# Two attention layers with routed experts on one core: VectorE subtracts the rotary products from batch 3 on

## The reference

```python
q = (x @ Wq + bq).reshape(Bx, Tx, NH, HD)      # 16 heads of 8
k = (x @ Wk + bk).reshape(Bx, Tx, NKV, HD)     # 4 heads of 8
x1, x2 = x[..., ::2], x[..., 1::2]             # rotary, for q and k
rot = concatenate([x1 * cos - x2 * sin, x1 * sin - x2 * cos], axis=-1)
scores = q @ k^T / sqrt(8), causal; softmax; @ v; @ Wo + bo
logits = norm(x) @ router_w.T + router_b       # top 2 of 8 experts for each token
out = sum over e of gate_e * (gelu(x @ up_w[e].T + up_b[e]) @ down_w[e].T + down_b[e])
```

## Time and profile before

| | |
|---|---|
| median of three runs | 530.03 us |
| runs | 530.03, 533.59, 527.95 us |
| the profiled execution: its own time | 533.82 us |
| its span, from the first to the last instruction | 532.1 us |
| granted TensorE clock, mean over the span | 0.956 |
| busy: TensorE, VectorE, ScalarE, GpSimd | 85%, 61%, 46%, 34% |
| GpSimd's rotations (L743) | 16 instructions, 11.3 us busy |
| GpSimd's scatters (L758) | 32 instructions, 31.1 us busy |

### The profile page before, as it was taken

The page is one execution under the profiler, slowest core; times in us unless marked ns, Lnnn a source line. Parts: engine busy times, 40 slices in busy tenths (PEclk is TensorE's granted clock), DMA queues, the critical chain, the costliest instruction groups (busy, mean ns, idle before and its releaser), DMA issues.

```text
span 532.1 us, 10260 instructions
## 1 busy us (share of the span) xinstructions
PE 451.8 (85%) x3455; PEld 338.5 (64%) x3455; DVE 323.5 (61%) x988; ACT 246.3 (46%) x561; POOL 182.4 (34%) x234
## 2 busy tenths in 40 slices
PE   1668899979999999998999968495979999999485
PEld 1544667758878877767656544254447999997243
DVE  5475641136767868868777875344456667775363
ACT  1821455435655555436545424233336555556152
POOL 6630110003435435444453443525231554443000
PEclk9999999988999999999999998788879999999699
DMA  5562124594224214112254330303032222112311
GB/s 161 145 211 62 63 63 118 150 162 124 75 52 125 86 42 123 45 37 79 84 158 161 78 105 16 117 3 122 8 110 65 54 73 71 56 46 80 114 43 41
DMA packets 48737, 46.96 MB, mean 88 GB/s; under 512 B 4976, under 2 KB 43520, under 8 KB 48688
## 3 DMA queue, kind: packets, MB, share of 16 engines
q1 hardware_dynamic: 44384, 35.12, 24.9%
q0 software_dynamic: 2576, 5.99, 3.5%
q10 hardware_dynamic: 1728, 5.23, 3.0%
HBM read 27.27 MB, written 19.04 MB: 87 GB/s over the span
## 4 chain that ended last, share of the span: by engine, by line
PE 68%; DVE 9%; issue 7%; DMA 4%; ACT 4%; another core or an unknown queue 3%; POOL 2%; SPq 1%; DVEq 0%; ACTq 0%; POOLq 0%
PE ps_S L1517 8%; PE ps_P L1539 7%; PE ps_N L1488 6%; PE ps_N L1671 5%; PE ps_N L1484 5%; PE ps_M L1712 3%; PE ps_P L1681 3%; PE ps_M L1681 3%; PE ps_M L1582 2%; PE ps_M L1619 2%; PE ps_P L1556 2%; PE ps_S L1671 2%; PE ps_P L1573 2%; DVE ROT L1096 2%
## 5 line engine op out<-in xcount | busy, mean ns | idle before, releaser
L839 ACT ACTIVATE PT<-ps_S 128x512 f32<-128x512 f32 x192 | 112.2, 592 | 118.5 <-PE ps_S L1517 92.8
L1067 DVE TENSOR_REDUCE NM<-ps_N 128x2 f32<-128x512 f32 (+1 forms) x192 | 128.2, 682 | 62.4 <-PE ps_N L1488 42.4
L1488 PE MATMUL ps_N<-STK 96*128 96x256 f32 (+1 forms) x256 | 104.3, 450 | 0.0
L701 POOL TENSOR_SCALAR_AFFINE_SELECT PT<-PT 128x512 f32<-128x512 f32 x80 | 49.1, 638 | 143.2 <-ACT PT L839 143.2
L1517 PE MATMUL ps_S<-STK 100*128 100x128 f32 (+5 forms) x352 | 94.1, 343 | 3.2 <-ACT PT L839 3.2
L1484 PE MATMUL ps_N<-maskb,identb 128*128 128x256 bf16 (+1 forms) x192 | 62.8, 327 | 5.9 <-DVE NM L1067 5.0
L1517 PEld LDWEIGHTS ps_S<-STK 104*128 104x128 f32 (+1 forms) x352 | 62.6, 199 | 7.4 <-ACT PT L839 4.4
L1539 PE MATMUL ps_P<-PT,VA 128*32 128x256 f32 (+1 forms) x1024 | 58.0, 346 | 0.4 <-ACT PT L839 0.4
L766 POOL DMA_INDIRECT yt<-LATE,EI x39 | 38.9, 998 | 55.9 <-DVE LATE L1307 45.5
L1488 PEld LDWEIGHTS ps_N<-STK 96*128 96x128 f32 x256 | 52.6, 206 | 4.9 <-issue 0.7
L1539 PEld LDWEIGHTS ps_P<-PT,VA 128*32 128x32 f32 x1024 | 27.6, 113 | 28.5 <-issue 14.8
(11 more groups left out here) (191 smaller groups left out, 790.6 us busy)
## 6 DMA issues: line engine op xcount, KB each, us to landing
STK<-scr SPq DMA_DIRECT2D x96, 96.0 KB
scr<-XQ SPq DMA_DIRECT2D x24, 256.0 KB
ROT<-in_L_ffn_W SPq DMA_DIRECT2D x16, 256.0 KB, 3.1
EW<-in_moe ACTq DMA_DIRECT2D x8, 512.0 KB, 3.4
scr<-XQ SPq DMA_DIRECT2D x24, 128.0 KB
xs<-zero SPq DMA_DIRECT2D x1, 2515.5 KB, 17.1
LATE<-xs SPq DMA_DIRECT2D x9, 258.0 KB
LATE<-yt SPq DMA_DIRECT2D x4, 512.0 KB, 5.7
```

Source lines behind the costliest of these rows:

```text
L701: last = pool.affine_select(out=v, in_=v, compare_op=ALU.is_ge, fill=0.0, base=0, pattern=[[0, 4], [1, P]], channel_multiplier=-1)
L839: act.activation(PT[:, g, r, :], bank[s][:], ACT.Exp, scale=SCALE).then_inc(exp_ok, 1)
L1067: dve.tensor_reduce(NM[b % 2][:, h, qt, :].rearrange("q (p c) -> q c p", p=2)[:, slots[0]:slots[-1] + 1, :], bank[s][:].rearrange("q (c p ...
L1488: last = mm(s[:, 2 * w_ * i:2 * w_ * (i + 1)], stk[0:QK_ROWS, c, P * qt:P * (qt + 1)], stk[0:QK_ROWS, k_slots(L, c, 2 * h, 2), 0:w_], star ...
```

## The change

From layer 1's batch 3 on, GpSimd's rotate returns at once, and VectorE does the two subtractions itself, right behind its products. It waits for its own products and for the count of the batch before, and then raises rsub_ok as GpSimd did. Batches 0 to 2 are as they were.

```diff
+ROT_DVE = 3
...
             def rotate(b):
 
                 n, i = b, b % 2
+                if n >= ROT_DVE:
+                    return
                 pool.wait_ge(rot_ok, n + 1)
                 for j, rows in ((0, P), (2, NKV * HD)):
                     last = pool.tensor_tensor(ROT[i][0:rows, j, :], ROT[i][0:rows, j, :], ROT[i][0:rows, j + 1, :],
...
                 last.then_inc(rot_ok, 1)
+                if b >= ROT_DVE:
+                    dve.wait_ge(rot_ok, b + 1)
+                    dve.wait_ge(rsub_ok, b)
+                    for j, rows in ((0, P), (2, NKV * HD)):
+                        last = dve.tensor_tensor(ROT[i][0:rows, j, :], ROT[i][0:rows, j, :], ROT[i][0:rows, j + 1, :],
+                                                 ALU.subtract)
+                    last.then_inc(rsub_ok, 1)
```

## The result

The changed kernel takes 545.05 us (median of 4 runs, 542.60 to 548.48), the kernel before 531.35 beside it (4 runs, 527.95 to 533.59): a ratio of 1.027, 95% interval 1.019 to 1.035. The prediction said 528.9 within 518 to 537. Time and sign are wrong. The profiled executions are 545.56 and 533.82 us, 11.7 apart. Some executions of any kernel here come out 1.5% or more above its fastest, and the profiled ones of keep_place (533.20 us) and of plain (519.16 us), further down, are of that kind, so that lengths read in them are compared with care.

What follows compares the result with a forecast made beforehand. It took TensorE, slowed by late signals during GpSimd's scatter bursts and the lowered clock after, as the bound. Terms -2.2 + 6.2 - 5.1 = -1.1 us, from the 530.03 us median to 528.9 us; range 518 to 537.

Steps and rivals of the forecast that it cites:

- Bound now: In t=12 to 15, GpSimd's back-to-back scatters delay TensorE's signals: 15.2 us lost to late signals, 10.7 to the clock.
- Rival C: Gaps in the passes aren't the scatters' doing and stay in t=14 and 15; only the subtract gains, 527.2 us; chance 0.13.
- The subtract: At pass heads, rotation ready 0.7 us earlier on VectorE, saving TensorE's 0.56 us wait in four passes: -2.2 us.
- The queues passed: In the rotation GpSimd issues only its two subtracts; no DMA moves on SP or ScalarE; no time term.
- the timing of the scatters: On GpSimd, two runs of 16 scatters 1.27 us apart, from about 310.4 until about 353; t=14 and 15 free.
- The scatters close up: In t=12 and 13, TensorE held 34.8 us at share 0.35, losing 21.4 us where it was 15.2: +6.2 us.
- rival B: In t=12 and 13, TensorE's signals stop altogether once a burst is long: +14.0 us held, 536.7 us; chance 0.20.
- A: Long scatter bursts hold TensorE no harder than short ones, share 0.57: -9.5 us, 520.5 us; chance 0.27.
- The clock: Half-clock stretches follow two held stretches instead of four, losing 5.6 us where it was 10.7: -5.1 us.

Runs made afterwards that it cites:

- keep_place: The changed kernel, but GpSimd still waits at its old place for VectorE's subtract, keeping scatter bursts of 6, 10, 9 and 7; 527.53 us, ratio 0.998.
- plain: The changed kernel without the sorting: GpSimd issues 32 plain DMAs of the same blocks back to back instead of indirect ones; 509.54 us, ratio 0.961.
- before_spaced: The kernel before, with GpSimd clearing 768 unused columns before each scatter; 513.34 us, 0.965 of the kernel before.
- spaced_384: The changed kernel, with GpSimd clearing 384 unused columns before each scatter, one every 1.57 us; 508.58 us, 0.958 of the kernel before.
- spaced: The changed kernel, with GpSimd clearing 768 unused columns before each scatter; 510.65 us, 0.962 of the kernel before.
- eights: The changed kernel, with GpSimd waiting for all landings after every eighth scatter; 531.12 us, 1.000 of the kernel before.

## Why the prediction was wrong

**Bound now: right in its core, one reading incomplete.** The gaps are the scatters' doing: with them spaced out and nothing else changed (before_spaced) the four passes of the kernel before go from 104.9 to 83.9 us, 21.0 less, and with the subtract on VectorE too (spaced_384) 27.8 less; the prediction's ledger had 15.2 + 10.7 = 25.9. Rival C is refuted, and with it what the prediction took from the Trainium skill ("SBUF — State Buffer", Who interferes with whom). The page says there that PE never waits on anyone, and here PE started 21 matmuls in 19.8 us beside GpSimd's scatters. The section is about SBUF's ports, and no run shows whether a port is what TensorE lacks. The incomplete reading is that "what is late is TensorE's own signal". Signals do come late: the matmul of 316.71 is over by 317.19, and the maximum that needs it starts at 332.94. But the matmuls themselves start late too, as the rows of 345.69 to 348.53 show.

**The subtract: right.** In t=11, where no scatter is, the pass took 298.92 - 278.61 = 20.3 us before and takes 298.59 - 278.96 = 19.6 now (products' starts in VectorE's timeline, the first row from the kernel before, the others after):

```profile
278.61 1.75 DVE L1096 SCALAR_TENSOR_TENSOR ROT<-ps_M,consts 128x256 f32<-128x256 f32 x4 [0.33 <-PE ps_M L1447]
```

```profile
278.96 1.75 DVE L1099 SCALAR_TENSOR_TENSOR ROT<-ps_M,consts 128x256 f32<-128x256 f32 x4 [0.33 <-PE ps_M L1457]
280.75 0.75 DVE L1108 TENSOR_TENSOR ROT<-ROT 128x256 f32<-128x256 f32 x2
```

That is 0.7 us; the subtracts start 0.04 us behind the products and take 0.75. The first maximum slid behind them (378.95), and TensorE has no new wait for it in the passes of t=14 and 15, 17.7 and 18.7 us long. In the whole time the 2.2 us that were forecast are too small to be shown: keep_place gains 1.1 us by the ratio (interval -3.3 to +1.1), and before_spaced against spaced some 1.5, with overlapping intervals.

**The queues passed, and the timing of the scatters: right.** Two runs of 16 from 311.45 to 353.4; "until about 353" it said. t=14 and 15: 36.4 us, said 38. Held time: 16.3 + 19.8 = 36.1 us, said 34.8.

**The scatters close up: this step failed.** It took TensorE's share in a long held stretch from the bursts of 9 and 10, 0.35 of the time busy, and kept it the same for 16: 34.8 us held, worth 13.4 us of work, 21.4 lost. By the matmuls that passed, the 36.1 us that were held are worth 6.1 us, a share of 0.17, and 30.0 are lost. That is rival B's 29.2, and its picture: next to nothing passes any more. The ledger of before was a little low too (15.2 lost; 28.8 - 10.75 = 18.05 by the same matching), so the term that was forecast at +6.2 measures 30.0 - 18.05, some +12.0: 5.8 us of the miss. The share falls with the length of the burst, as eights shows with the pace unchanged. The prediction had even seen the lateness grow within one burst, 2.3 and then 6.1 us, used it in the rivals (against A, for B), and then took the mean of the two longest bursts where the trend had to be carried on to 16.

**The clock: half of the gain.** -5.1 us rested on two slow stretches in place of four, 10.7 us long. The granted clock is 0.50 for 44.4 us, from 320.5 to 364.9, where the passes of before have 27.3 in four pieces. It lasts on through the break (332.9 to 337.3) and 7.8 us into t=13, which therefore took 19.4 us and not 17.7. What the passes lost outside the held stretches was 27.75 - 18.05 = 9.7 us and is 37.1 - 30.0 = 7.1: 2.6 less, and in it is the subtract's gain of three passes (1.7 forecast), so clock and subtract together are forecast -6.8 and measured -2.6. That is 4.2 us of the miss. What half clock costs inside a held stretch isn't shown by itself; it is in the share of 0.17.

**The experts: not looked at.** The prediction put nothing on the experts. Their part of the span grew from 128.3 to 130.95 us, and it is the granted clock at its start. The first 54 matmuls of it, between the same two instructions of VectorE, first before and then after:

```profile
403.81:411.12 7.31, 6.55 (x54) 6.10 (x55) 5.28 (x21) 4.79 (x14) 0.96 (x1) 1.00 0.14 37
...
412.85:422.55 9.70, 9.19 (x54) 8.78 (x55) 5.27 (x20) 3.42 (x12) 0.96 (x1) 0.66 0.14 36
```

That is 2.4 of the 2.7 us, at the level of 1.2 GHz for 6.8 us. Just ahead of it stands a new wait, for the load of the sorted rows:

```profile
412.85 0.17 DVE L1308 SCALAR_TENSOR_TENSOR aside<-LATE,consts 128x4 f32<-128x4 f32 x1 [2.73 <-DMA LATE<-xs]
```

SP issued that load at 409.99, behind its last row of the passes, although the last row of the scatters had landed by 354.3. Before, no such wait stood there (0.67 us, "issue"). The wait itself ends at 412.85 and so lies inside the pass of t=15, which is 18.7 us and not 17.7; it can't be part of the 2.7 behind it. Nor is it shown to bring the half clock: spaced_384 has the same wait (2.58 us), starts its experts at full clock and needs 7.18 us for the same matmuls. Why the clock is low here stays open.

The sum: held +5.8, clock and subtract +4.2, experts +2.7, and 0.2 in t=11, against a miss of 11.7 + 1.1 = 12.8 (the rest is rounding).

**The rivals.** B was the case, with the chance of 0.20 that I gave it; priced at 536.7, it too fell short, because it kept the clock's -5.1 us and put nothing on the experts. The prediction's own bound, slower by over 1% once the share is below about 0.18, is where the kernel came out. A is refuted by the change itself (t=12 and 13 at 77.9 us; A said under 60).

**What stays open.** What it is in GpSimd's handling of an indirect DMA that slows TensorE. It isn't bytes, rows, direction, DRAM writes, the loading of instructions, or 16 DMAs issued by GpSimd as such. That it behaves like something that fills up (a pace that it can bear between 1.4 and 1.57 us, a longer burst holding harder) fits the rows of the table; relief comes near the landing, 0.5 us behind the last packet in the first run of 16 and 2.8 behind it in the second. The thing itself is not shown. Bursts of plain DMAs longer than 8.6 us were not tried, and nor was a burst of six or more from SP.

## What to carry to other kernels

An engine's idle wait between its DMAs may be what paces them: before it is removed, ask what the burst without it does to the others, and carry a trend within one burst on to the longer one rather than averaging it. When signals end long waits as "remote" while another engine issues indirect DMAs back to back, space these out first (here 4% for a clearing of 384 columns, or for a wait on work that the plan has anyway). A term for the clock is only as good as the term for the idle time that it follows. And compare work by the same instructions in two traces: at half clock an engine is busy for longer with less.

## What the runs showed of the hardware

- GpSimd's indirect DMAs, back to back at 1.27 us (0.96 busy, 0.30 gap), slow TensorE from the third to fifth on, down to one matmul per 1.4 us in a burst of 16, with weight loads and matmuls starting on a beat of 0.70 us. At 1.57 us apart no slowing shows, at 1.4 TensorE is slowed in part, at 1.14 more.
- 33 values a row instead of 129, 16 rows instead of 128, or a gather instead of a scatter don't end it (30 to 41 us lost, after 37); 16 plain DMAs from GpSimd in 8.6 us don't cause it.
- Breaks shorten it: two waits for all landings, 1.57 and 1.95 us, took 14 us off the time. It can outlast the last packet, by 2.8 us in the kernel after, with no DMA moving.
- In the kernel after the granted clock stays at half for 44.4 us, from 3.9 us into the first held stretch to 7.8 us behind the second.
